# Two issuing queues for the adjacency load of a two-layer graph kernel: groups 2 and 3 of each quarter move to ACT's queue

## The chip, the cores and the metric

The kernel runs on 1 core of a Trainium2 chip. The metric is the device time of one execution in microseconds, as the median of several runs. Engines: PE (TensorE), PEld (its weight loads), DVE (VectorE), ACT (ScalarE), POOL (GpSimd) and SP (SyncE, which only issues transfers here). ACT, POOL and SP each issue transfers into a queue of their own: q1 is SP's, q10 ACT's, q0 POOL's.

## The reference, cut to what matters

N = 4096 nodes, D = 256 features, `adj` is a 4096 x 4096 int32 matrix of zeros and ones (67 MB), W matrices are 256 x 256 or 512 x 256:

```
h    = relu(layernorm(x))
mask = adj > 0;  deg = sum(mask, axis=1)
agg  = mask @ h / max(deg, 1)
x    = x + relu(concat(h @ W_self + b_self, agg @ W_nb + b_nb) @ W_comb + b_comb)
h    = relu(layernorm(x))
Wh   = (h @ W) in 4 heads of 64;  sl, sr = Wh . a_l, Wh . a_r
e    = leaky_relu(sl[i] + sr[j]), where adj or i == j, else -inf
x    = x + elu(softmax(e) @ Wh)
```

## The kernel before, in words

The kernel has three stages. In the first (up to about 75 us) the first layer's normalised h is multiplied with weights folded beforehand, for 16 pairs of row tiles; results stay in SBUF as `g`. In the second (about 75 to 345 us) the adjacency matrix is multiplied with `g`, one row tile of 128 rows at a time, 32 tiles t. The third (from about 345 us) is the attention layer over the stored mask. The change touches the second.

**How the matrix comes in.** It is read as 64 quarters of 1 MB, n = 0 to 63; four of them make a pair of row tiles. A quarter goes to a slot: a part of the later mask that is not yet in use, or one of three spare buffers (`stage`, `stage2`). `adj_rows(eng, n, parts)` (L330) waits until the slot is free and issues one transfer of 256 KB for each partition group a of `parts`: group a is the 32 partitions from 32 a on, with two pieces of 4 KB in each. Before, SP issues all four groups of a quarter in the order 0, 2, 1, 3, one quarter behind the other (L378 to L381). `slot_free` (L310) waits for the quarter that used the slot before, `LAST_IN[n]`, to be converted (`bits_ready`): for n = 21 to 33 that is quarter n - 13, for 34 to 41 quarter n - 10, then ever nearer, n - 3 for the last two. Quarters 17 to 20 have slots that no quarter used before.

**What is done with a quarter.** DVE converts it to bytes (`to_bits`, L984, the instruction at L989) and turns it in 32 x 32 blocks into the mask (`turn`, L993, the instruction at L996). In tile t DVE converts quarters 2t + 6 and 2t + 7.

**A tile t on the engines.** PE adds up the tile's product with the mask (`sums`, L587 and L589), in the middle of it transposes h1 of the tile before (`turn_h1`, L599) and at its end multiplies it with the second layer's weights (`wh_product`, L608). `sums` waits for the mask of its rows and for x1 of the tile two before. DVE's `post(t)` (L999) computes x1 (L1018, L1020), its statistics (L1023, L1027), converts the first quarter, computes the factors (L1030, L1031), then turns that quarter, converts the second, takes the low part of the transposed h1 (`low_h1T`, L1037) and turns the second. L1018 writes into one of two x1 buffers and waits until the store of x1 from that buffer, two tiles before, has landed (`x1_out`).

ACT works through this list for each tile, in order (written out in its program, L757 to L763): `norm1` (root L736, h1 L740, x1 - 1 L743), `store_x1` (L340, 128 KB from the x1 buffer to scratch memory), `high_h1T` (L747, copy of the transposed h1), `copy_wh` (L753, L754, copy of the product), `store_wh` (L345, 128 KB). So ACT's queue carries two stores a tile. `copy_wh` waits for the store of wh two tiles before. POOL loads, for each tile, its part of the first layer's own term and of x.

Of the kernel before, what the change touches and what calls it, by code (L numbers as in the profile page):

```python
# [41 lines left out]
NT = 2 * NK  # L42
# [27 lines left out]
def build(nc, x, adj, W_self, b_self, W_nb, b_nb, W_comb, b_comb, W, a_l, a_r, out):  # L70
# [15 lines left out]
    with ExitStack() as ctx:  # L86
# [223 lines left out]
        def slot_free(eng, n):  # L310

            if n == EARLY:
                eng.wait_ge(wmm_ready, 2)
            elif n == EARLY + 1:
                eng.wait_ge(ab_ready, 4)
                eng.wait_ge(consts, 5)
            elif n == EARLY + 2:
                eng.wait_ge(h_ready, NK)
            elif n == EARLY + 3:
                eng.wait_ge(hT_ready, NK)  # L320
            elif n in (EARLY + 7, EARLY + 8, EARLY + 9):
                eng.wait_ge(mm_free, 2 * NK + 4)
            elif n == EARLY + 10:
                eng.wait_ge(mm_free, 2 * NK + 4)
                for b in range(2):
                    eng.wait_ge(own_out[b], 16 * NP2)
            elif n > EARLY:
                eng.wait_ge(bits_ready, LAST_IN[n] + 1)

        def adj_rows(eng, n, parts):  # L330

            slot_free(eng, n)
            for a in parts:
                eng.dma_start(slots[SLOT[n]][a * UP:(a + 1) * UP, :].rearrange("p (e c) -> p e c", e=2),  # L334
                              adj_v[n // UN, n % UN, a]).then_inc(raw_in[SLOT[n]], 16)

        def store_x1(eng, t):

            eng.wait_ge(x1m_ready, t + 1)
            eng.dma_start(x1_d[t], x1[:, t % 2, :]).then_inc(x1_out[t % 2], 16)  # L340

        def store_wh(eng, t):

            eng.wait_ge(wh_ready, t + 1)
            eng.dma_start(wh_d[t], wh[:, t % 2, :]).then_inc(wh_out[t % 2], 16)  # L345
# [11 lines left out]
        def _(sp):  # L357
# [20 lines left out]
                x_rows(sp, k, (0, 2), x_in)  # L378
                adj_rows(sp, (k - 1) // 3, ((0, 2), (1,), (3,))[(k - 1) % 3])
            for n in range(NK // 3, 2 * NT):  # L380
                adj_rows(sp, n, (0, 2, 1, 3))  # L381

            sp.wait_ge(s0_out, 16)
            sp.wait_ge(turned, NT * 2)
# [297 lines left out]
        def _(act):  # L682
# [51 lines left out]
            def norm1(t, e):  # L734
                act.wait_ge(var1_ready, t + 1)
                nc.scalar.activation(std1[:, :], mv1[:, 1:2], ACT.Sqrt, bias=eps[:, 0:1]).then_inc(std1_ready, 1)  # L736
                act.wait_ge(norm1_ready, t + 1)
                if t >= 2:
                    act.wait_ge(h1T_ready, t - 1)
                nc.scalar.activation(h1[:, e, :], x1[:, e, :], ACT.Relu, bias=shift1[:, 0:1], scale=rstd1[:, 0:1]  # L740
                                     ).then_inc(h1_ready, 1)

                nc.scalar.activation(x1[:, e, :], x1[:, e, :], ACT.Copy, bias=-1.0).then_inc(x1m_ready, 1)  # L743

            def high_h1T(t, e):
                act.wait_ge(h1T_ready, t + 1)
                nc.scalar.activation(h1T[:, e, 0, :], ps_h[:, 0:D], ACT.Copy).then_inc(h1T_high, 1)  # L747

            def copy_wh(t, e, k):
                act.wait_ge(wh_mm_ready, t + 1)  # L750
                if k:
                    act.wait_ge(wh_out[e], k * 16)
                nc.scalar.activation(wh[:, e, :], ps_w[:, 0:D], ACT.Copy, scale=VSCALE / WSCALE).then_inc(wh_ready, 1)  # L753
                nc.scalar.activation(sr[:, t:t + 1, :], ps_w[:, D:E1].unsqueeze(1), ACT.Copy,  # L754
                                     scale=1.0 / WSCALE).then_inc(sr_ready, 1)

            for t in range(NT - 2):  # L757
                norm1(t, t % 2)
                store_x1(act, t)
                high_h1T(t, t % 2)  # L760
                copy_wh(t, t % 2, t // 2)
                store_wh(act, t)
                if t == NJ + 1:  # L763
                    act.wait_ge(s0T_ready, 1)
                    nc.scalar.activation(s0_row.rearrange("q (n e) -> q e n", e=2),
                                         ps_s0.rearrange("q (e n) -> q e n", e=2), ACT.Copy).then_inc(s0_ready, 1)
# [101 lines left out]
        def _(dve):  # L868
# [406 lines left out]
            for gr in range(1, NG):  # L1275

                heads = gr % NS == 0
                for q in range(NQ):
                    z_of(gr, q)
                    signs(gr, q + 1)  # L1280
                    if q == 1 and not reads_early(gr):
                        read_plus(gr - 1)
                    if q == (4 if heads else 2):
                        sums(gr - 1)
                    if q == (5 if heads else 3):
                        denominators(gr - 1)
                        divide(gr - 1)
                    if q == (7 if heads else 6):
                        add_x1(gr - 1)
                    if q == 7:  # L1290
                        finish(gr - 1)
                    for n in pieces_at(gr, q):
                        products(n)
                    for n in pieces_at(gr, q - 1):
                        highs_of(n)
                        lows(n)
                    pos_of(gr, q)
                    if q == 0 and reads_early(gr):
                        if gr == 1:
                            dve.wait_ge(fac_halved, 1)  # L1300
                        read_plus(gr - 1)
# [22 lines left out]
EARLY = 10  # L1324


def raw_slots():

    slot = [NK, NK + 1, NK + 2] + list(range(1, 8)) + [8, 10, 15, 11, NK, NK + 1, NK + 2, 14, 13, 9, 12]
    last_in = [None] * len(slot)  # L1330
    for n in range(len(slot)):
        last_in[n] = max([m for m in range(n) if slot[m] == slot[n]], default=-1)
    for n in range(len(slot), 2 * NT):
        held = {}
        for m in range(n):
            held[slot[m]] = m
        m, free = min((m, r) for r, m in held.items() if r >= NK or UN * r > n)
        slot.append(free)
        last_in.append(m)
    return slot, last_in  # L1340


SLOT, LAST_IN = raw_slots()


def reads_early(gr):


    return gr % NS in (0, 1)
# [53 lines left out]
```

## Time and profile before

| | us |
|---|---|
| median of 3 runs | 835.57 |
| lowest, highest | 832.29, 836.24 |
| the profiled execution | 840.03 |
| its span | 838.2 |

| engine | busy us | share of the span |
|---|---|---|
| PE | 789.9 | 94% |
| DVE | 695.5 | 83% |
| ACT | 563.5 | 67% |
| POOL | 144.0 | 17% |

The profile is taken from one execution; its times start at the span's start. q1 (SP's queue) carried 92.50 MB, q0 (POOL's) 14.17 and q10 (ACT's) 8.39. In the page's forty slices of 21 us each the DMA engines are busy nearly without a pause in the first fifteen, and hardly after it; PE is near 9 tenths in nearly all. The whole span's shares mix three stages, so each stage is to be read by itself, in windows.

### The profile page before, as it was taken

Reading aid. Unit: us, or ns where it says so; the run is one execution under the profiler, and the core shown is the slowest. Engines: PE = TensorE matmul, PEld = TensorE weight load, DVE = VectorE, ACT = ScalarE, POOL = GpSimd, SP = SyncE. Lnnn points to the kernel's source line nnn. Section 1 sums busy time; section 2 is a strip of 40 time slices with the busy share of each in tenths; the row PEclk is TensorE's granted clock in tenths of the full one; section 3 lists DMA queues with packets and bytes.
Section 4 is the critical chain, followed back from the end, with each engine's and each line's share of the span. In section 5 each row is a group of like instructions: output and inputs, shape, how many; then the busy total and the mean of one; then the engine's idle time right before and its main releaser. Section 6 shows DMA issues by size and latency. Waiting matters only on the chain.

```text
span 838.2 us, 26127 instructions
## 1 busy us (share of the span) xinstructions
PE 789.9 (94%) x10791; PEld 724.3 (86%) x10791; DVE 695.5 (83%) x1339; ACT 563.5 (67%) x841; POOL 144.0 (17%) x215
## 2 busy tenths in 40 slices
PE   6888999998999999699999999999999999999995
PEld 4335888877888888489999999999999999999995
DVE  4998877766677774788889999879998889998884
ACT  4663222222222222889999989999989999999991
POOL 2631645533435542000000000000000000000000
PEclk9999999999999999699999999999999999999998
DMA  9989999999999993400411101410110311022001
GB/s 240 277 248 281 288 295 290 276 282 285 321 350 348 333 294 106 111 2 26 82 29 40 50 7 43 100 50 0 50 50 18 83 50 45 5 50 51 13 13 38
DMA packets 95748, 115.68 MB, mean 138 GB/s; under 512 B 61580, under 2 KB 71504, under 8 KB 95696
## 3 DMA queue, kind: packets, MB, share of 16 engines
q1 hardware_dynamic: 78416, 92.50, 40.2%
q0 software_dynamic: 7712, 14.17, 5.7%
q10 hardware_dynamic: 9568, 8.39, 3.5%
q8 instruction: 23, 0.38, 0.2%
q14 instruction: 29, 0.24, 0.1%
HBM read 98.17 MB, written 16.85 MB: 137 GB/s over the span
## 4 chain that ended last, share of the span: by engine, by line
PE 52%; DVE 18%; SPq 9%; ACT 8%; DMA 7%; issue 5%; POOL 1%; DVEq 0%; ACTq 0%
PE ps_x L649 9%; PE ps_a L649 9%; PE ps_t L649 9%; SPq L334 9%; PE ps_t L587 7%; PE ps_t L589 7%; ACT stage L778 6%; PE ps_w L649 4%; PE ps_h L649 4%; DVE stage L1098 4%; DMA stage<-in_adj 3%; DMA mask<-in_adj 2%; DVE stage L1088 2%; DVE stage L1109 2%; DMA own_scratch<-mask 1%
## 5 line engine op out<-in xcount | busy, mean ns | idle before, releaser
L587 PE MATMUL ps_t<-g,mask 128*128 128x257 f16 x1024 | 227.9, 273 | 3.1 <-DVE mask L996 3.1
L589 PE MATMUL ps_t<-g,mask 128*128 128x256 f16 x1024 | 227.9, 272 | 0.0
L778 ACT ACTIVATE stage<-rows,sr 128x1024 int8<-128x1024 f32 x192 | 204.2, 1171 | 5.7 <-PE ps_w L649 5.7
L778 ACT ACTIVATE stage<-bits,sr 128x1024 int8<-128x1024 f32 x192 | 204.3, 1167 | 2.7 <-PE ps_w L649 2.7
L1098 DVE SCALAR_TENSOR_TENSOR stage<-stage,mask 128x1024 int32<-128x1024 int32 x128 | 156.7, 1224 | 21.5 <-ACT stage L778 21.0
L649 PE MATMUL ps_x<-g,stage 128*128 128x130 f16 x2048 | 159.1, 220 | 10.6 <-DVE stage L1109 4.7
L649 PE MATMUL ps_t<-g,stage 128*128 128x130 f16 x2048 | 158.8, 220 | 0.0
L649 PE MATMUL ps_a<-g,stage 128*128 128x130 f16 x2048 | 158.6, 220 | 0.0
L649 PEld LDWEIGHTS ps_x<-g,stage 128*128 128x128 fp8e4 x2048 | 127.5, 98 | 12.8 <-issue 12.6
L649 PEld LDWEIGHTS ps_t<-g,stage 128*128 128x128 fp8e4 x2048 | 127.5, 97 | 0.2
L649 PEld LDWEIGHTS ps_a<-g,stage 128*128 128x128 fp8e4 x2048 | 127.3, 97 | 0.1
L587 PEld LDWEIGHTS ps_t<-g,mask 128*128 128x128 fp8e4 x1024 | 99.8, 97 | 17.3 <-issue 3.9
L589 PEld LDWEIGHTS ps_t<-g,mask 128*128 128x128 fp8e4 x1024 | 99.7, 97 | 11.7
L1109 DVE TENSOR_SCALAR stage<-stage 128x1024 int32<-128x1024 int32 x128 | 88.6, 692 | 18.5 <-PE ps_w L649 18.1
L483 POOL DMA_DIRECT2D rows<-in_x x128 | 100.1, 788 | 0.7 <-issue 0.6
L649 PE MATMUL ps_w<-g,stage 128*128 128x130 f16 x1024 | 100.1, 220 | 0.0
L649 PE MATMUL ps_h<-g,stage 128*128 128x130 f16 x1024 | 100.0, 220 | 0.0
L649 PEld LDWEIGHTS ps_h<-g,stage 128*128 128x128 fp8e4 x1024 | 68.5, 97 | 0.1
L649 PEld LDWEIGHTS ps_w<-g,stage 128*128 128x128 fp8e4 x1024 | 68.4, 97 | 0.1
L753 ACT ACTIVATE late<-ps_w 128x256 f32<-128x256 f32 x32 | 12.2, 383 | 80.8 <-PE ps_w L608 80.8
L989 DVE TENSOR_SCALAR bits<-mask 128x2048 uint8<-128x2048 int32 x38 | 46.4, 1220 | 13.1 <-DMA mask<-in_adj 13.1
L1088 DVE TENSOR_SCALAR stage<-bits,sr 128x1024 uint8<-128x1024 f32 x64 | 48.3, 756 | 0.0
(135 smaller groups left out, 801.8 us busy)
## 6 DMA issues: line engine op xcount, KB each, us to landing
mask<-in_adj SPq DMA_DIRECT2D x152, 256.0 KB, 20.0
stage<-in_adj SPq DMA_DIRECT2D x104, 256.0 KB, 16.1
own_scratch<-mask POOLq DMA_DIRECT2D x16, 256.0 KB, 4.6
rows<-own_scratch POOLq DMA_DIRECT2D x32, 128.0 KB, 6.9
rows<-in_x POOLq DMA_DIRECT2D x128, 32.0 KB, 6.7
bits<-s_scratch SPq DMA_DIRECT2D x8, 512.0 KB, 4.1
rows<-s_scratch SPq DMA_DIRECT2D x8, 512.0 KB, 4.7
late<-x_scratch SPq DMA_DIRECT2D x16, 256.0 KB, 3.1
```

The lines of the kernel that those rows point to most:

```text
L334: eng.dma_start(slots[SLOT[n]][a * UP:(a + 1) * UP, :].rearrange("p (e c) -> p e c", e=2), adj_v[n // UN, n % UN, a]).then_inc(raw_in[SLOT ...
L483: pool.dma_start(xt[a * UP:(a + 1) * UP, e, :], x_v[a, t // 2, :, e * D:(e + 1) * D]).then_inc(row_in[e], 16)
L587: nc.tensor.matmul(ps_t32[e][:, 0:D + 1], at, g[:, 2 * kk + b, D:2 * D + 1], start=kk + b == 0, stop=kk == NK - 1 and b == 1, skip_group_c ...
L589: last = nc.tensor.matmul(ps_t32[e][:, 0:D], at, g[:, 2 * kk + b, 0:D], start=False, stop=kk == NK - 1 and b == 1, skip_group_check=True)
L649: last = nc.tensor.matmul(acc[j][:, br * VBLK:(br + 1) * VBLK], bytes_of(ring[:, q % size, j // 2, k % 2, :], j % 2, b), val[:, 2 * k + b, ...
L753: nc.scalar.activation(wh[:, e, :], ps_w[:, 0:D], ACT.Copy, scale=VSCALE / WSCALE).then_inc(wh_ready, 1)
L778: nc.scalar.activation(sign_bytes(sgn, k, b), srow[gr % 2].rearrange("p (r n) -> p r n", n=2 * P), ACT.Sign, bias=sr[:, 2 * k + b, H + gr ...
L989: nc.vector.tensor_scalar(bits[:, n % 2, :].rearrange("p (m e s) -> p e m s", e=2, s=2), slots[SLOT[n]].rearrange("p (e m s) -> p e m s", ...
L1088: nc.vector.tensor_scalar(sign_bytes(sgn, k, 1).bitcast(U8), srow[gr % 2].rearrange("p (r n) -> p r n", n=2 * P), sr[:, 2 * k + 1, 2 * H + ...
L1098: nc.vector.scalar_tensor_tensor(sg, sg, SIGN_BITS, mask32[:, strip:strip + NJ // 2, 2 * q:2 * q + 2, :] .rearrange("p r k n -> p r (k n)" ...
L1109: nc.vector.tensor_scalar(pos[:, q % PR, :, :, :].rearrange("p r k n -> p (r k n)"), sgn[:, q % ZR, :, :, :].rearrange("p r k n -> p (r k ...
```

## The change

SP issues the four groups of a quarter only up to quarter 17, and from 18 on groups 0 and 1 alone. Groups 2 and 3 of these are issued by ACT, at two places of its list for a tile: behind `store_x1` and behind `high_h1T`. A step is one such place, 2t for the first and 2t + 1 for the second. `issued_at(step)` gives the quarters of a step: the next one or two whose slot's last user has a number of at most step + 6. It gives 18 and 19 at step 0, 20 to 33 one at each of the steps 1 to 14, none at 15 to 17, 34 to 41 one at each of the steps 18 to 25, and the others at most one a step, 63 at step 54. Bytes, slots and destinations stay the same.

```diff
             for n in range(NK // 3, 2 * NT):
-                adj_rows(sp, n, (0, 2, 1, 3))
+                adj_rows(sp, n, (0, 2, 1, 3) if n < EARLY + 8 else (0, 1))
...
             for t in range(NT - 2):
                 norm1(t, t % 2)
                 store_x1(act, t)
+                for n in issued_at(2 * t):
+                    adj_rows(act, n, (2, 3))
                 high_h1T(t, t % 2)
+                for n in issued_at(2 * t + 1):
+                    adj_rows(act, n, (2, 3))
                 copy_wh(t, t % 2, t // 2)
                 store_wh(act, t)
...
+def issued_at(step):
+
+    done = EARLY + 8
+    for now in range(step + 1):
+        new = [n for n in range(done, min(done + 2, 2 * NT)) if LAST_IN[n] <= now + 6]
+        if now == 0:
+            new = [n for n in new if n < EARLY + 10]
+        done += len(new)
+    return new
```

## Rows read from the trace of the kernel before

**Rows 1.** Windows of the second stage: busy us and count by engine, PE clock, DMA share, GB/s.

```profile
80.00:120.00 40.00, 40.00 (x365) 35.42 (x364) 32.70 (x68) 9.36 (x27) 22.20 (x26) 1.00 1.04 290
120.00:170.00 50.00, 50.00 (x457) 44.36 (x455) 37.81 (x85) 13.03 (x38) 26.47 (x32) 1.00 1.05 283
170.00:210.00 40.00, 35.42 (x314) 29.80 (x312) 26.01 (x60) 8.63 (x26) 13.77 (x21) 1.00 1.04 284
250.00:290.00 40.00, 40.00 (x366) 35.51 (x365) 31.23 (x70) 10.21 (x30) 20.06 (x25) 1.00 1.04 348
```

**Rows 2.** Chain of waits (start us, us, what); then ACT's copies from 138 to 241.

```profile
90.48 0.69 PE ps_w L608 x6
98.41 0.69 PE ps_w L608 x6
138.02 0.69 PE ps_w L608 x6
240.65 0.86 PE ps_w L608 x6
...
L753 ACT ACTIVATE late<-ps_w x12: 383/383/384, 138.7 to 233.3; 128x256 f32<-128x256 f32 x12
```

**Rows 3.** Waits from 170 to 240 us: who for whom, total, times, longest.

```profile
DVE bits L989 <- DMA mask<-in_adj: 12.2, 10, 2.8
DVE bits L989 <- DMA stage<-in_adj: 6.4, 5, 2.3
```

**Rows 4.** DMA queues from 80, 120 and 250 us: packets, MB, share; landing.

```profile
q1 hardware_dynamic: 2759, 9.04, 81.7%
q10 hardware_dynamic: 1011, 0.92, 8.5%
...
q1 hardware_dynamic: 3262, 10.68, 78.9%
mask<-in_adj SPq DMA_DIRECT2D x31, 256.0 KB, 22.2
...
q1 hardware_dynamic: 3403, 11.14, 81.8%
q10 hardware_dynamic: 1529, 1.39, 10.9%
```

**Rows 5.** The chain of waits, two of SP's issues.

```profile
156.42 2.56 SPq L334
159.03 0.59 SPq L334
```

**Rows 6.** Timeline of ACT, tiles 0 and 1; last row DVE's, tile 1.

```profile
88.54 0.38 ACT L747 ACTIVATE late<-ps_h 128x256 f16<-128x256 f32 x1 [0.43 <-PE ps_h L599]
95.06 0.34 ACTq L340 DMA_DIRECT2D x_scratch<-late  x1
96.25 0.38 ACT L747 ACTIVATE late<-ps_h 128x256 f16<-128x256 f32 x1 [1.22 <-PE ps_h L599]
99.13 0.38 ACT L753 ACTIVATE late<-ps_w 128x256 f32<-128x256 f32 x1 [2.50 <-PE ps_w L608]
...
96.67 0.42 DVE L1037 TENSOR_TENSOR late<-ps_h,late 128x256 f16<-128x256 f32 x1 [0.84 <-ACT late L747]
```

**Rows 7.** An x1 store (ACT), its landing, and the buffer's next writer (DVE).

```profile
126.91 0.33 ACTq L340 DMA_DIRECT2D x_scratch<-late  x1
...
x_scratch<-late ACTq DMA_DIRECT2D x1, 128.0 KB, 9.1
...
138.60 0.48 DVE L1018 SCALAR_TENSOR_TENSOR late<-ps_t,deg,rows 128x256 f32<-128x256 f32 x1 [0.18 <-DVE deg L1010]
```

**Rows 8.** DMA queues from 128 to 131 us, then from 250 to 252.

```profile
q1 hardware_dynamic: 182, 0.59, 66.9%
q10 hardware_dynamic: 144, 0.13, 16.3%
...
q10 hardware_dynamic: 139, 0.13, 18.8%
```

## The prediction

> **What bounds the kernel now.** I read the windows of the stage first [rows 1]. From 80 to 170 us PE is busy all the time; from 170 to 210 only 35.42 of 40 us; from 250 to 290 it is busy throughout again. The DMA engines are full all along (1.04), but move 283 to 290 GB/s at first and 348 from 250 on. So this stage has two bounds: PE, and where PE has gaps the stream of adjacency quarters. The chain of waits gives PE's pace: the product of one row tile starts at 98.41 and that of the fifth after it at 138.02, 7.92 us a tile. A later row of the same kind stands at 240.65; ACT copies each product 0.7 us behind it, and made 12 such copies between 138.7 and 233.3, the first of them that of 138.02 [rows 2]. So 240.65 is 12 tiles on: 12 x 7.92 = 95.0, the clock says 102.6, and 7.6 us are lost. The waits of 170 to 240 us name the reason [rows 3]: DVE waits 12.2 and 6.4 us, 15 times, for landed quarters, and PE needs the mask that DVE makes of them.
>
> The queue rows show how fast quarters come [rows 4]: SP's queue q1 moved 9.04 MB in the 40 us from 80 (226 GB/s) and 10.68 MB in the 50 from 120 (214). A quarter is 1.049 MB, thus 4.6 to 4.9 us, and PE eats two in 7.92 us, 3.96 each. From 250 on it is 11.14 MB in 40 us (279 GB/s), 3.8 us each. Landing takes 22.2 us at 214 GB/s, which is 4.75 MB or 18 transfers of 256 KB: SP's queue is full, its issues grow from 0.59 to 2.56 us because of that, and not because SP is slow [rows 4, 5].
>
> **What the change removes and adds.** Per quarter SP issues two transfers less, ACT two more. SP's time is worth nothing: its issues are long only because the queue is full. The most that can come back on the PE side is the 7.6 us, and only if the quarters land earlier. What is lost near the end of the stage is not counted.
>
> ACT's issuing time: 0.59 us plus 0.04 to the next, as SP's short ones [rows 5], so 1.26 us per quarter. At the first place of a tile they stand between the x1 store and the copy of the transposed h1. In tile 1 the store's issue ends at 95.40, the copy starts at 96.25 after 1.22 us of idle [rows 6]: it becomes 0.4 us late. DVE waits 0.84 us for it anyway, PE needs the result at about 98.4, and the two steps take 0.8 us: covered by 1.0 us. At the second place (after the copy, before the product's copy) ACT idles 2.50 us, again more than 1.26. These two cost nothing. In tile 0 the first place issues quarters 18 and 19, four transfers, 2.5 us: the copy, now at 88.54 right behind the store's issue, then starts at 91.0 in place of 88.54, with DVE's 0.42 us PE's product starts at 91.8 and not 90.5: +1.4 us, once. The waits for free slots are met: at the first place the quarter asked for was converted before the norm's factors; at the second DVE converts it just ahead of the step that waits for ACT's copy.
>
> What is not covered lies behind the queue. ACT's queue also carries x1 and wh to scratch, and a queue is served in order. The x1 store issued at 126.91 must have landed before DVE writes that buffer again at 138.60, 11.69 us later; a store of that stretch took 9.1 us [rows 7]. Margin 2.6 us. (The wh buffers are asked for at a later point of the tile and are left out.) Now each tile puts four adjacency transfers in front of the next x1 store. How fast does a second queue drain beside SP's full one? In the 3 us in which one store is served (128 to 131 us), q1 has 182 packets and q10 144 [rows 8]: nearly one for one. That is 9 packets per engine, 0.33 us for each of ACT's 1 KB packets. The packet's own time: q10 8.5% of 16 x 40 us over 1011 packets is 0.054, with the 1 in 9 that only reports landing taken out 0.06; q1 81.7% over 2759 packets, 1 in 5 taken out, 0.24 us for 4 KB [rows 4]. So an adjacency packet in ACT's queue costs 0.33 + 0.18 = 0.51 us. A tile has 2 stores of 8 packets per engine and 4 transfers of 4: 16 x 0.33 + 16 x 0.51 = 13.4 us, against 7.92. At the packet times seen from 250 us on (139 packets in 2 us, 0.23 us; q1's packet 0.19, q10's 0.05) it is 16 x 0.23 + 16 x 0.37 = 9.6 us [rows 4, 8]. Either way ACT's queue gets behind, x1 lands late, DVE's next x1 waits, and behind it stand the conversion of quarters and all PE needs. The tile then takes what the queue takes.
>
> How long: as long as SP's queue is full. At 88.5 us it holds 18 transfers, 72 packets per engine, of quarters before 18. Served at 1 to 1.26 of ACT's 32 a tile (I take 36), they last 2 tiles. Here SP's queue still alternates over all groups, as before, so 13.4 us: 2 x 5.5 = +11 us. Then SP runs through its halves (8 packets a quarter) until the slots stop it: a slot is free 13 quarters behind the last converted one (7 at the start, 2 more each tile). 72 + 8 x (2 + 2T) = 36T gives T = 4.4 tiles, so 2.4 more. At 9.6 us they cost +4, at 13.4 +13; I take +8, since the shorter packets were seen only with a single full queue. From then on SP only follows the slots, ACT's queue drains, and PE, by then late, finds its data there: the 7.6 us of starvation is gone.
>
> Sum: 1.4 + 11 + 8 - 2.6 (margin) - 7.6 = +10.2 us. With 9.6 us throughout: 4.4 x 1.7 - 2.6 - 7.6 = -2.7. With 13.4 throughout: 1.4 + 24 - 2.6 - 7.6 = +15; if nothing of the starvation returns, +23. The profiled execution took 840.03 us (span 838.2 and 1.8 around it), 4.5 above the median of 835.57; I put the difference on the median: 846.
>
> Two rules of the Trainium skill bear on this, in opposite senses. The row first: q1 ran at 214 to 226 GB/s while its queue was full [rows 4]. "SBUF — State Buffer" (Door 1: the DMA port swizzle) says that 32 partitions reach 8 of the 16 ports, with an asymptote of 218 GB/s, and that groups 0 and 1 share one set of ports, 2 and 3 the other. The early rows agree, those from 250 on (279) do not stay under it. By this rule two queues, each on its own ports, could move more than one, and the first rival below gets its strength. "DMA: Bandwidth & Descriptors" (Rules for kernel authors) says that spreading DMAs over issuing engines does not help bandwidth, it saves issuing time only; by it nothing would be gained, which is the third rival's case.
>
> **Rivals.** (1) Faster. The two queues together reach 348 GB/s as in 250 to 290 from the start, a quarter needs 3.8 us, the DVE waits of [rows 3] vanish, and ACT's stores pass in time because the packets of other groups do not block one another. Place: tiles 11 to 19; it decides from about 165 us; price -7.6: 828 us. For it: the higher rate exists in the same kernel [rows 1]. Against it: one-for-one service makes ACT's 32 packets a tile need more than a tile even at the fast packet times. (2) Slower by ACT's own time. If the queue of ACT fills up, its issues become as long as SP's, up to 2.56 us [rows 5]; two of them before the copy then overrun the 2.1 us from 95.40 to 97.5, the time at which the copy must start [rows 6], by up to 3 us, say 1.5 on 16 tiles: +24 - 7.6 = +16, 852. Against it: the x1 buffer stops ACT before 18 transfers are waiting. (3) No change. The engines move the same bytes at the same rate, early stalls only take the place of the later ones: 836, within 4.
>
> **Chances.** My forecast 0.60 (own range 833 to 851; 0.04 of it faster, 0.06 within 0.5%, 0.50 slower), rival 1 0.20, rival 2 0.12, rival 3 0.08. 0.5% is 4.2 us, about what can be told from no change here. Faster 0.24, same 0.14, slower 0.62. The range is 827 to 858: its foot takes in the upper half of rival 1, its head +22.
>
> **What would show it.** Profile after, right: DVE L1018 (the x1 step) waits for an x1_scratch landing between 100 and 160 us, x1 stores land after 12 to 20 us in place of 9, PE has its gaps there and none from 170 to 240; DVE's waits for in_adj nearly gone; SP's issues short; q10 carries some 32 MB. The last tile's product stands some 10 us later, the later stages unchanged in length. Wrong: x1 stores still land within 11 us while q10 carries adjacency packets; then service isn't one for one, or the packets are much faster, and the time goes to 828. If L1018 waits but the total is the same or lower, the size of the slow stretch (4.4 tiles) is wrong. If the copy of h1 (L747) is what PE waits for, it is rival 2.

## The result, and the profile after

The changed kernel takes 872.93 us (median of 4 runs, 867.86 to 874.04) against 834.88 before: a ratio of 1.0442 (95% interval 1.0396 to 1.0488), slower by 38 us where +10 had been forecast, and outside the range. The profiled execution took 873.3 us with a span of 871.5, 33.3 more than the 838.2 of before.

Against the profiled executions the difference is 33.3 and against the medians 38, because the profiled execution of before was itself some 5 us slower than its median. All of it lies in the second stage. The last product of that stage starts at 375.46 us, before at 342.21, which is 33.25 later. The chain of waits of the kernel after, rows of the products (start us, us, what), and ACT's copies of them (count, then first and last start):

```profile
92.83 0.86 PE ps_w L608 x6
187.87 0.69 PE ps_w L608 x6
241.23 1.21 PE ps_w L608 x6
362.42 0.69 PE ps_w L608 x6
375.46 1.53 PE ps_w L608 x6
...
L753 ACT ACTIVATE late<-ps_w x8: 383/384/384, 101.7 to 188.6; 128x256 f32<-128x256 f32 x8
L753 ACT ACTIVATE late<-ps_w x6: 383/383/384, 196.7 to 242.5; 128x256 f32<-128x256 f32 x6
L753 ACT ACTIVATE late<-ps_w x17: 364/383/384, 250.4 to 377.0; 128x256 f32<-128x256 f32 x17
```

Counted by the copies, these are the products of tiles 0, 8, 14, 29 and 31. At 7.92 us a tile [rows 2] tiles 0 to 8 should take 63.4 us and took 95.0: 31.7 lost. Tiles 8 to 14 took 53.4 in place of 47.5: 5.8 lost. Tiles 14 to 29 took 121.2 in place of 118.8: 2.4 lost. Tile 0 starts 2.35 us later than before [rows 2]. That makes 42.2; the kernel before lost 7.6 up to its tile 18 and 1.2 after it, and 42.2 - 8.8 is 33.4, where 33.25 was seen.

The windows of the kernel after (columns as in [rows 1]) show where. PE has gaps in each of them, most of all up to 170 us. Up to 170 us the DMA share is as full as before, at 266 and 285 GB/s (290 and 283 before); from 170 us on both share and rate are lower than before.

```profile
80.00:120.00 40.00, 32.85 (x298) 28.62 (x295) 24.61 (x54) 6.42 (x19) 15.03 (x18) 0.99 1.04 266
120.00:170.00 50.00, 37.84 (x288) 30.27 (x288) 23.09 (x52) 7.87 (x23) 16.07 (x19) 0.87 1.04 285
170.00:210.00 40.00, 35.01 (x297) 30.12 (x298) 28.04 (x62) 9.77 (x28) 21.87 (x26) 0.91 0.95 248
210.00:250.00 40.00, 35.99 (x310) 30.73 (x309) 25.47 (x58) 8.55 (x25) 17.35 (x21) 0.96 0.98 254
250.00:290.00 40.00, 39.63 (x361) 34.97 (x359) 29.81 (x66) 10.21 (x30) 21.33 (x25) 1.00 1.00 257
```

The waits of the kernel after between 80 and 360 us name what the engines now wait for (who, for whom, total, times, longest). In [rows 3] DVE waited for `in_adj`; no such row is left. L1022 is L1018 of before, the x1 step.

```profile
DVE late L1022 <- DMA x_scratch<-late: 35.5, 9, 8.5
ACT late L753 <- DMA wh_scratch<-late: 32.9, 6, 8.3
PE ps_h L599 <- ACT late L740: 26.0, 7, 7.3
```

The chain of waits (first rows) goes through such stores: the one issued at 134.94 lands 20.92 us later (9.1 in [rows 7]), and right behind it, at 156.09, DVE starts the x1 step that needs the buffer. The two rows behind the first break are the x1 steps of 130.79 and 143.86 in DVE's timeline, the last two the queues from 120 to 140 us.

```profile
105.67 24.89 DMA x_scratch<-late
134.94 20.92 DMA x_scratch<-late
156.09 0.49 DVE late L1022
160.25 20.89 DMA x_scratch<-late
...
130.79 0.48 DVE L1022 SCALAR_TENSOR_TENSOR late<-ps_t,deg,rows 128x256 f32<-128x256 f32 x1 [3.95 <-DMA x_scratch<-late]
143.86 0.48 DVE L1022 SCALAR_TENSOR_TENSOR late<-ps_t,deg,rows 128x256 f32<-128x256 f32 x1 [5.40 <-DMA x_scratch<-late]
...
q1 hardware_dynamic: 956, 3.15, 57.5%
q10 hardware_dynamic: 948, 1.95, 37.6%
```

The two x1 steps of the timeline are 13.1 us apart: that is the tile, no longer 7.92. The queues were served 956 to 948 packets.

From 101.5 to 181.4 us the three landings are 66.7 of the chain's 79.9 us; the rest are the steps of DVE and ACT from one x1 to its store, and no product of PE is in it. So PE's clock, whose mean falls to 0.87 in the window from 120 us, is not what makes these tiles long. Later it costs a little: from 238.88 to 241.23 us the chain does run over PE's products, at 0.21 us each, the lower of its two levels (1.2 and 2.4 GHz), in place of 0.11, and the second layer's product at 241.23 takes 1.21 us in place of 0.69. That is some 1.7 us by an estimate from these rows.

### The profile page after: what moved, and what is told of

Its sections match the earlier page's. It is cut to its first block, busy times and chain, and to the rows that moved or that the text cites. A ratio compares the mean times of both kernels' runs of the same rounds, so it can differ in the third digit from the quotient of the medians.

```text
span 871.5 us, 26128 instructions
## 1 busy us (share of the span) xinstructions
PE 798.6 (92%) x10791; PEld 728.2 (84%) x10791; DVE 694.1 (80%) x1339; ACT 563.5 (65%) x841; POOL 155.4 (18%) x215
## 4 chain that ended last, share of the span: by engine, by line
PE 48%; DVE 20%; DMA 12%; ACT 12%; issue 5%; ACTq 1%; POOL 1%; DVEq 0%; SPq 0%
DMA x_scratch<-late 9%; ACT stage L782 9%; PE ps_x L649 9%; PE ps_a L649 8%; PE ps_t L649 8%; PE ps_t L587 6%; PE ps_t L589 6%; PE ps_w L649 4%; PE ps_h L649 4%; DVE bits L993 3%; DVE stage L1102 3%; DMA own_scratch<-mask 2%; ACTq L334 1%; PE ps_w L608 1%; DVE stage L1092 1%
## 5 line engine op out<-in xcount | busy, mean ns | idle before, releaser
L587 PE MATMUL ps_t<-g,mask 128*128 128x257 f16 x1024 | 234.6, 278 | 3.0 <-DVE mask L1000 2.9
L589 PE MATMUL ps_t<-g,mask 128*128 128x256 f16 x1024 | 234.4, 277 | 0.0
L587 PEld LDWEIGHTS ps_t<-g,mask 128*128 128x128 fp8e4 x1024 | 101.5, 99 | 18.8 <-issue 3.7
L589 PEld LDWEIGHTS ps_t<-g,mask 128*128 128x128 fp8e4 x1024 | 101.6, 99 | 13.5
L483 POOL DMA_DIRECT2D rows<-in_x x128 | 112.3, 883 | 0.7 <-issue 0.6
L753 ACT ACTIVATE late<-ps_w 128x256 f32<-128x256 f32 x32 | 12.2, 383 | 83.5 <-PE ps_w L608 50.6
L736 ACT ACTIVATE std<-mv,eps 128x1 f32<-128x1 f32 x32 | 9.4, 295 | 65.2 <-DVE mv L1031 65.2
L1092 DVE TENSOR_SCALAR stage<-rows,sr 128x1024 uint8<-128x1024 f32 x64 | 48.1, 751 | 0.0
```

The source lines that it names most:

```text
L483: pool.dma_start(xt[a * UP:(a + 1) * UP, e, :], x_v[a, t // 2, :, e * D:(e + 1) * D]).then_inc(row_in[e], 16)
L587: nc.tensor.matmul(ps_t32[e][:, 0:D + 1], at, g[:, 2 * kk + b, D:2 * D + 1], start=kk + b == 0, stop=kk == NK - 1 and b == 1, skip_group_c ...
L589: last = nc.tensor.matmul(ps_t32[e][:, 0:D], at, g[:, 2 * kk + b, 0:D], start=False, stop=kk == NK - 1 and b == 1, skip_group_check=True)
L1092: nc.vector.tensor_scalar(sign_bytes(sgn, k, 1).bitcast(U8), srow[gr % 2].rearrange("p (r n) -> p r n", n=2 * P), sr[:, 2 * k + 1, 2 * H + ...
```

## The experiments

Two theories after the result. Q: the x1 and wh stores stand behind quarters in ACT's queue. R: two queues, split by halves of the partitions, are slower as such. A third, P, came from the first run. Line numbers shift by some lines from kernel to kernel; the text says which step is meant.

**Stores in POOL's queue.** In the changed kernel:

```diff
 # POOL, in its loop over the tiles
                     row(t + 2)
+                    store_x1(pool, t)
+                    if t:
+                        store_wh(pool, t - 1)
 # ACT (and SP for the last two tiles)
-                store_x1(act, t)
-                store_wh(act, t)
```

> The change as it is, but the x1 and wh stores are issued by POOL's queue, no longer behind ACT's adjacency transfers. Theory Q (the loss of 37 us is the x1 and wh stores standing behind ACT's adjacency transfers): the stores land in 8 to 12 us again, DVE L1022's wait for them (35.5 us) goes under 5, total 832 to 845. Theory R (two queues, each with its own half of the partitions, lower the rate of all transfers): total stays at 862 to 875, the waits are only named differently.

850.82 us, ratio 1.0207 (1.0144 to 1.0270). By the ratios 20 of the 37 us are gone, which R does not explain, and 17 are left, more than Q said. An x1 store issued from 100 to 140 us lands after 11.4 us, and DVE waits for x1 stores 1.1 us in all. What stops DVE now stands in its timeline in this run, the conversions (L995, L989 of before) of quarters 15, 16 and 17, and in the chain of waits, which reaches the third of them over a single landing of a quarter's group:

```profile
128.38 1.23 DVE L995 TENSOR_SCALAR bits<-stage 128x2048 uint8<-128x2048 int32 x1 [3.67 <-DMA stage<-in_adj]
138.73 1.23 DVE L995 TENSOR_SCALAR bits<-stage 128x2048 uint8<-128x2048 int32 x1 [5.79 <-DMA stage<-in_adj]
147.56 1.23 DVE L995 TENSOR_SCALAR bits<-mask 128x2048 uint8<-128x2048 int32 x1 [6.72 <-DMA mask<-in_adj]
...
103.37 44.17 DMA mask<-in_adj
...
mask<-in_adj SPq DMA_DIRECT2D x17, 256.0 KB, 37.6
mask<-in_adj ACTq DMA_DIRECT2D x12, 256.0 KB, 22.4
```

The two last rows are landings of transfers issued from 100 to 140 us: SP's now take 37.6 us (22.2 before [rows 4]), ACT's 22.4. Served in turn, ACT's halves of quarters from 18 on, which are needed only some 50 us after they are asked for, hold up the whole quarters 15 to 17 in SP's queue, which are needed first. That is theory P.

**Control: the kernel before, with the same move of the stores.**

> The kernel before, with the x1 and wh stores issued by POOL's queue. It is the control of the run above: what moving the stores costs or gains by itself. Both theories: 833 to 842; POOL's issues are longer than ACT's (0.57 to 0.93 against 0.33 us), and POOL has room for them.

836.32 us, ratio 1.0038 (1.0006 to 1.0070): the move itself costs about 3 us.

**Groups 0 and 2 on SP, 1 and 3 on ACT.**

```diff
-                adj_rows(sp, n, (0, 2, 1, 3) if n < EARLY + 8 else (0, 1))
+                adj_rows(sp, n, (0, 2, 1, 3) if n < EARLY + 8 else (0, 2))
-                    adj_rows(act, n, (2, 3))
+                    adj_rows(act, n, (1, 3))
```

> The change, but SP brings groups 0 and 2 from quarter 18 on, ACT groups 1 and 3, so that each queue has both halves of the partitions. Theory Q: the early stall is the same (13 us a tile for some 6 tiles), total 860 to 875. Theory R: packets get shorter, the 250 to 290 us windows show well under 1.00 DMA share at the same GB/s, and the total falls by 10 us or more.

871.41 us, ratio 1.0442 (1.0370 to 1.0514): the same as the change itself (872.93, ratio 1.0442). Which halves of the partitions a queue has does not decide.

**ACT takes over from quarter 34 only.**

```diff
-                adj_rows(sp, n, (0, 2, 1, 3) if n < EARLY + 8 else (0, 1))
+                adj_rows(sp, n, (0, 2, 1, 3) if n < 34 else (0, 1))
-    done = EARLY + 8
+    done = 34
```

> The change, but ACT takes over only from quarter 34, when SP's issues follow the slots and its queue is no longer full for long. Theory Q: the long stall from 100 to 183 us is gone, stores land in under 13 us, total 832 to 846. Theory R: the slower packets of the later part remain, starvation from 170 us on grows, total 845 to 860.

849.45 us, ratio 1.0176 (1.0114 to 1.0238). Q had said at most 846, R 845 to 860. The stall moved with the takeover: from 155 to 215 us DVE waits 10.3 us for x1 stores, and an x1 store takes 16.3 us. I had been wrong that SP's queue is no longer full by then: SP's issues from 144 to 169 us, in which time ACT began, took 1.1 us each (0.59 where they are short [rows 5]).

**ACT late, stores in POOL's queue.** The test of P, on top of the first run:

```diff
-        new = [n for n in range(done, min(done + 2, 2 * NT)) if LAST_IN[n] <= now + 6]
+        new = [n for n in range(done, min(done + 2, 2 * NT)) if LAST_IN[n] <= now + 6 and n <= now + 12]
```

> The run with the stores in POOL's queue took 851 us: 22 of the 38 us were the stores. In its trace the quarters 15 to 17, which SP issues whole, land at 128, 139 and 148 us in place of 110, 114 and 119 before, while ACT's halves of 18 and later land 50 us before they are used. Here ACT asks for quarter n at step n - 12 at the earliest, 6 steps before its use. Theory P (the other part of the loss is ACT's early halves taking turns with SP's whole quarters, which are needed first): DVE's 16.6 us of waits for quarters 15 to 17 go, total 834 to 842. Theory R (two queues are slower as such): the waits move to quarters after 27, total stays at 845 to 855.

835.39 us, ratio 1.0007 (0.9990 to 1.0025): P holds. ACT's queue still brings half of each of 46 quarters, and it costs nothing. The windows of 120 to 170 and 170 to 210 us of this run:

```profile
120.00:170.00 50.00, 50.00 (x457) 44.37 (x456) 38.26 (x85) 12.82 (x38) 34.19 (x45) 1.00 1.03 322
170.00:210.00 40.00, 40.00 (x366) 35.53 (x364) 31.30 (x72) 10.65 (x31) 26.84 (x38) 1.00 1.04 323
```

PE has no gap, at 322 GB/s over two queues and POOL's. From 120 to 170 us the queues were served 1937 to 1941 packets, so service in turn is still there. R as a cause of the loss is out.

**From quarter 34, stores in POOL's queue.**

> ACT takes over from quarter 34 only, and the stores are in POOL's queue: neither stores behind quarters nor early halves beside whole ones that are needed first. Theories Q and P: 832 to 842, as the control with the stores in POOL's queue. Theory R: the packets of 4 KB take 0.25 us from quarter 34 on in place of 0.19, and starvation from 200 us on costs 5 to 15 us: 842 to 852.

856.88 us, ratio 1.0268 (1.0222 to 1.0314): outside what P and Q said and above R's range too, and above the run with the stores left on ACT. The waits from 155 to 215 us (who, for whom, total, times, longest) again name quarters, not stores:

```profile
DVE bits L995 <- DMA mask<-in_adj: 12.3, 4, 4.9
DVE bits L995 <- DMA stage<-in_adj: 11.6, 3, 5.1
...
mask<-in_adj SPq DMA_DIRECT2D x19, 256.0 KB, 28.5
mask<-in_adj ACTq DMA_DIRECT2D x7, 256.0 KB, 10.4
```

The last rows are landings from 160 to 200 us. SP's queue held the whole quarters before 34, already late in this run, and ACT's halves overtook them. I read it as P once more: what counts is the backlog of whole quarters in SP's queue, and that this combination would avoid it was my error. This reading rests on the waits and the landings; no run with a later start tests it here.

**ACT late, stores on ACT.** The same condition as above, on the changed kernel itself.

> The change as it is (x1 and wh stores in ACT's queue) with one condition more: ACT asks for quarter n at step n - 12 at the earliest. With the stores in POOL's queue this gave 835 us. Theory Q (stores behind quarters in one queue cost time as long as SP's queue is full, whatever the quarters' date): SP's halves run ahead until quarter 34, so x1 stores land in 15 us or more between 110 and 160 us, total 845 to 860. Theory P (ACT's early start is all): 833 to 840.

861.59 us, ratio 1.0312 (1.0274 to 1.0350): as Q said, a little above. From 110 to 160 us an x1 store lands after 16.0 us, a wh store after 19.7.

**x1 stores in POOL's queue, wh stores on ACT.**

> The change with the x1 stores in POOL's queue and the wh stores left in ACT's, behind the quarters. The prediction left the wh stores out. If they do not matter: as with both stores in POOL's queue, 849 to 853. If they hold the tile too (ACT L753 waited 26.8 us for their landing in the changed kernel, 16.6 us even with both in POOL's queue): 858 to 870, with PE waiting through the copy of the product.

857.52 us, ratio 1.0254 (1.0198 to 1.0309); the 1.0207 with both on POOL lies just inside its lower end, the 1.0442 with both on ACT does not. By the ratios moving x1 saves 16 us of 37, moving wh too saves 4 more, within the uncertainty. But the trace shows what holds the tiles once x1 is out of the way: ACT waits 71.9 us, 11 times, for wh stores, and from 94 to 180 us the chain of waits goes over four landings of wh stores, 20.3 to 22.8 us each.

**The order of groups in the kernel before.**

```diff
-                adj_rows(sp, n, (0, 2, 1, 3))
+                adj_rows(sp, n, (0, 1, 2, 3))
```

> The kernel before with SP's order of groups 0, 1, 2, 3 in place of 0, 2, 1, 3: two transfers in turn to the same half of the partitions. If a half of the partitions is a limit of its own (the 214 to 226 GB/s of the rows before), the packets get longer and the total goes up by 3 to 15 us; if not, 831 to 838.

864.09 us, ratio 1.0321 (1.0270 to 1.0373), more than expected. From 120 to 170 us q1 moves 10.27 MB, 205 GB/s, and the windows of this run stay at 268 to 287 GB/s from 80 to 320 us.

**The kernel before again.**

> The kernel before again, for a second trace of it: all theories give 832 to 838. Open is whether 4 KB packets again need 0.24 us up to about 217 us and 0.19 from there on, or whether that point moves from run to run, as the trace with ACT from quarter 34 makes likely (there it lay at about 115 us, with the same instructions up to then).

834.01 us, ratio 0.9996 (0.9973 to 1.0019). Its trace, windows from 80, 120, 170 and 250 us and the queues of 120 to 170:

```profile
80.00:120.00 40.00, 40.00 (x361) 35.32 (x360) 31.58 (x68) 8.47 (x25) 19.93 (x23) 0.99 1.04 323
120.00:170.00 50.00, 50.00 (x457) 44.40 (x456) 38.39 (x86) 13.56 (x39) 27.84 (x33) 1.00 1.04 371
170.00:210.00 40.00, 40.00 (x366) 35.53 (x364) 30.70 (x69) 10.51 (x31) 22.56 (x28) 1.00 1.00 310
250.00:290.00 40.00, 40.00 (x366) 35.52 (x364) 31.01 (x70) 10.21 (x30) 21.02 (x25) 1.00 1.05 286
...
q1 hardware_dynamic: 4653, 15.25, 84.0%
```

The same program, the same instructions: 371 GB/s where [rows 1] have 283, and no gap of PE. The 7.6 us of starvation belong to the one execution that was profiled: it took 840.03 us, this one 834.12, and the medians of before (833 to 836) lie with the second.

The runs that vary ACT's start and the stores' queue, as us above the kernel before that ran beside them (ratio less 1, times 834; each is uncertain by 2 to 5 us):

| | stores on ACT | stores on POOL |
|---|---|---|
| ACT from step 0 (quarter 18) | +37 | +17 |
| ACT at step n - 12 at the earliest | +26 | +1 |
| ACT from quarter 34 | +15 | +22 |

## Why the prediction was right and wrong

- **Direction and mechanism: right.** The step "what is not covered lies behind the queue" named the x1 store, the x1 step on DVE and service in turn. The trace has all three, and moving the stores, with ACT late, takes the loss from +26 to +1.
- **Service of the two queues: right.** "1 to 1.26" packets of SP for one of ACT; measured 956 to 948. A tile at "13.4 us"; the x1 steps stand 13.1 us apart. The stores land later than was named: 20.9 to 24.9 us, where "12 to 20" stood.
- **Tile 0, "+1.4 us": right.** The product of tile 0 is 2.35 us later. Of this 0.7 was there before ACT's first issue (the first conversion of the tile starts at 86.39 in place of 85.67), which leaves 1.6.
- **The step that failed: the length and the price of the slow stretch, the terms +11 and +8.** "2.4 more tiles" at "+8" rested on the short packets of [rows 4] from 250 us on. They never came: q1's 57.5% of 16 x 20 us over 956 packets, with 1 in 5 taken out, is 0.24 us. And the stretch was not 4.4 tiles long: at one for one the same equation, 88 + 16T = 32T, gives 5.5, and DVE's x1 steps show six tiles of 12.2 to 16.3 us. Six times 13.3 - 7.92 is 32 us; the two terms and the margin (11 + 8 - 2.6) said 16.4, and 31.7 was measured. (The low bound, -2.7, also leaves out the 1.4 of tile 0; with it, it is -1.3.)
- **"The 7.6 us of starvation is gone": failed as a gain.** The waits for quarters went as named, but in their place tiles 8 to 14 lose 5.8 us, as ACT's queue falls behind again between 210 and 250 us (an x1 store issued at 217.48 lands after 15.88 us), and tiles 14 to 29 lose 2.4. "None from 170 to 240" was wrong: PE is busy 35.01 and 35.99 of 40 us there. And [rows 3] had been read as the kernel's loss; the second trace of it has none. The prediction saw that the profiled execution was 4.5 us slower than the median, and still took the 7.6 off the median. "If nothing of the starvation returns, +23" was the end of the bounds, and with the stretch's real length it would have been +31.
- **The wh stores, "left out": wrong.** They are waited for 32.9 us in all. In the changed kernel the chain of waits from 101.5 to 181.4 us goes over the x1 stores; with x1 alone moved it goes over the wh stores instead, and the total stays 21 us above the kernel before.
- **Not foreseen: the order of need.** That ACT's early halves delay SP's whole quarters is not seen in the changed kernel (DVE has no wait for `in_adj` there), where the x1 wait slows the tiles and hides it, and costs some 17 us as soon as the stores are out of the way. The two effects do not add: 26 for the stores alone and 17 for the early halves alone, together 37.
- **Rival 1** is false for the change. Two queues can come near its 348 GB/s: 322 with the stores elsewhere and late starts. Rival 2 did not decide: most of ACT's issues stayed at 1.2 us a pair, and PE's wait for ACT L740 is the x1 wait handed on. But its mechanism is there in small: before the copy of h1 at 288.77, 312.95 and 329.47 us ACT's pair took 2.0 to 2.3 us, and the products of these three tiles come 0.4 to 0.7 us late each, 1.6 of the 2.4 us that tiles 14 to 29 lose.
- **The two rules.** The row first: with successive transfers to one half of the partitions q1 moves 204 to 223 GB/s in the windows from 80 to 290 us, and the kernel loses 27 us. The Trainium skill, "SBUF — State Buffer" (Door 1), gives an asymptote of 218 GB/s to 32 or 64 partitions of one half; the run agrees within 7%. Giving each queue a half of its own brought nothing: 872.93 us, and 871.41 with both halves in each. The other row: with all queues together 322 GB/s were moved where SP and ACT share the quarters, and 283 and 371 in the two traces in which SP brings them alone; the medians of the two kernels are both 834 to 835 us, so spreading brought nothing. The Trainium skill, "DMA: Bandwidth & Descriptors" (Rules for kernel authors), says that it does not help bandwidth; the runs agree.

What stays open: what sets the length of a packet. The same program moved 274 to 300 GB/s up to some 210 us and more behind it in one execution, and about 370 from 105 to 185 us and 286 from 250 to 290 in another. Packets of 4 KB are longer late in the changed kernel (0.26 us from 250 to 290, by q1's 37.6% of 16 x 40 us over 1159 packets, 1 in 5 taken out) than in the one with late ACT and stores on POOL (0.21 from 120 to 170, by 40.2% of 16 x 50 us over 1937). But this is not the change's doing alone: in the second trace of before the same working gives 0.18 us from 120 to 170 (84.0% over 4653) and 0.24 from 250 to 290 (78.6% over 2605). No version beat the kernel before.

## What to carry to other kernels

Before work moves to another engine's queue, list what that queue already carries and when each transfer must have landed; a small store with 2.6 us of margin becomes the bound as soon as bulk loads stand before it. Two full queues are served in turn whatever is urgent: a queue that is asked early for late data takes half of the service from the one that is asked late for urgent data, so ask by date of need. And take a second trace of the kernel before the change, before a wait in it is counted as a gain to be had.

## What the runs showed of the hardware

- Two full queues were served one packet for one: 956 to 948 packets from 120 to 140 us in the changed kernel, 1270 to 1277 from 100 to 140 with the stores on POOL.
- Order within one queue: 0, 1, 2, 3 in place of 0, 2, 1, 3, groups of 32 partitions, cost 3.2%; from 120 to 170 us q1 moved 205 GB/s against 214 and 305 in the two traces of the usual order.
- The same program in two executions: 283 and 371 GB/s in the window of 120 to 170 us, at a DMA share of 1.05 and 1.04. A full share does not say that the rate is at its limit.
- PE's granted clock had a mean of 0.87 in the changed kernel's window of 120 to 170 us, in which PE was idle a quarter of the time, and of 1.00 in the windows without gaps of the run with late ACT and stores on POOL.
